# Output weights of twelve heads, the output bias and the first quad's queries moved from the attend block into the queries stage

## What is computed

```python
# layer 1; x is (16, 128, 512), context (16, 128, 512), 16 heads of 128
h = layernorm(x)
q = rms_norm(h @ q_w + q_b, nq_s)            # heads: "queries stage"
k = rms_norm(context @ ki_w + ki_b, nki_s)   # computed long before
v = context @ vi_w + vi_b                    # computed long before
p = softmax(q @ k.T / sqrt(128))             # per batch and head
x = x + (p @ v) @ o_w + o_b                  # o_w: 2048 x 512, sixteen heads
h = layernorm(x)
s = mean(abs(weight))
x = x + h @ (s * clip(round(weight / s), -1, 1)).T + bias
```

## Time and profile before

| | us |
|---|---|
| median of 3 runs | 1416.97 (1416.31 to 1417.77) |
| the profiled execution, its time | 1421.35 |
| its span, first to last instruction | 1419.6 |
| TensorE busy | 1335.0 (94%) |
| VectorE busy | 832.8 (59%) |
| ScalarE busy | 769.9 (54%) |
| GpSimd busy | 411.6 (29%) |
| mean granted TensorE clock | 0.966 |

### The profile page before, as it was taken

The page is one execution under the profiler, slowest core; times in us unless marked ns, Lnnn a source line. Parts: engine busy times, 40 slices in busy tenths (PEclk is TensorE's granted clock), DMA queues, the critical chain, the costliest instruction groups (busy, mean ns, idle before and its releaser), DMA issues. The chain is left out here.

```text
span 1419.6 us, 24647 instructions
## 1 busy us (share of the span) xinstructions
PE 1335.0 (94%) x7326; PEld 1117.0 (79%) x7327; DVE 832.8 (59%) x1575; ACT 769.9 (54%) x1890; POOL 411.6 (29%) x387
## 2 busy tenths in 40 slices
PE   6899989999999889989998989999958999999998
PEld 5688868888888767768886668888857888888887
DVE  2545533667676775354444458633258877777866
ACT  3325445788887542154446534545457566665661
POOL 0111023373739003559631054030056100000031
PEclk9999987999999999999999989999979999999999
DMA  6994479878787457476657877474446655556413
GB/s 231 357 350 163 147 236 294 283 247 292 260 268 254 174 141 289 178 227 179 198 144 238 282 237 228 110 243 147 158 146 165 167 157 165 159 162 164 119 45 119
DMA packets 175095, 288.33 MB, mean 203 GB/s; under 512 B 30176, under 2 KB 64736, under 8 KB 174752
## 3 DMA queue, kind: packets, MB, share of 16 engines
q1 hardware_dynamic: 149200, 231.78, 52.2%
q0 software_dynamic: 8672, 29.37, 6.4%
q10 hardware_dynamic: 17136, 26.09, 5.0%
HBM read 178.38 MB, written 108.80 MB: 202 GB/s over the span
## 5 line engine op out<-in xcount | busy, mean ns | idle before, releaser
L2778 ACT ACTIVATE attend_prob<-banks,attend_row,rq 128x128 f32<-128x128 f32 x256 | 113.7, 454 | 51.0 <-DVE attend_row L2853 50.9
L109 PE MATMUL banks<-of_shared_split,heads_wl 128*128 128x512 f32 x256 | 109.0, 426 | 9.2 <-ACT heads_ksq L1002 5.2
L109 PE MATMUL banks<-attend_wol,attend_ol 128*128 (+1 forms) x256 | 106.0, 414 | 0.0
L111 PE MATMUL banks<-of_shared_split,heads_wt 128*128 128x512 f32 x256 | 103.2, 403 | 0.0
L110 PE MATMUL banks<-of_shared_split,heads_wl 128*128 128x512 f32 x256 | 103.1, 403 | 0.0
L109 PE MATMUL banks<-queries_rows_split,queries_wl 128*128 128x512 f32 x256 | 100.8, 394 | 0.0
L111 PE MATMUL banks<-attend_wol,attend_ot 128*128 (+1 forms) x256 | 100.7, 393 | 0.0
L111 PE MATMUL banks<-queries_rows_split,queries_wt 128*128 128x512 f32 x256 | 99.8, 390 | 0.0
L110 PE MATMUL banks<-attend_wot,attend_ol 128*128 (+1 forms) x256 | 99.8, 390 | 0.0
L110 PE MATMUL banks<-queries_rows_split,queries_wl 128*128 128x512 f32 x256 | 99.7, 390 | 0.0
L2463 DVE TENSOR_TENSOR queries_total<-queries_total,queries_sq 128x512 f32<-128x512 f32 x60 | 41.6, 693 | 90.0 <-ACT queries_sq L2391 90.0
(11 more groups left out here) (374 smaller groups left out, 3660.9 us busy)
## 6 DMA issues: line engine op xcount, KB each, us to landing
mlstm_gmax<-running_max SPq DMA_DIRECT2D x36, 512.0 KB, 6.4
heads_raw<-in_L_xattn_ki_w SPq DMA_DIRECT2D x32, 512.0 KB, 6.4
k_heads<-heads_key ACTq DMA_DIRECT2D x64, 256.0 KB, 4.8
q_heads<-queries_head SPq DMA_DIRECT2D x64, 256.0 KB, 2.9
attend_q<-q_heads SPq DMA_DIRECT2D x64, 256.0 KB, 4.1
of_attend_k<-k_heads SPq DMA_DIRECT2D x60, 256.0 KB, 4.0
of_attend_v<-v_heads SPq DMA_DIRECT2D x60, 256.0 KB, 3.4
sorted_rows<-of_shared_split SPq DMA_DIRECT2D x2, 5120.0 KB, 30.0
```

What stands on the lines that cost most here:

```text
L109: nc.tensor.matmul(out, lead_l, lead_r, start=first, stop=False)
L111: return nc.tensor.matmul(out, trail_l, lead_r, start=False, stop=last)
L2778: ins = nc.scalar.activation(prob[:, j % 2, b, :], ps[:, j % 2, b * S:(b + 1) * S], ACT.Exp, bias=row[:, j % 2, 1, b:b + 1], scale=rq[:, b ...
```

## The change

Three pieces of work move from the start of the attend block into the queries stage.

The tile of the output weights becomes one, `wo`, with lead and trail of a head side by side, 2 KB apart, at the address of `rows_split`, the split normalised rows. These rows are free group by group as the last heads pass, and four heads of weights fit in the place of one group. So ScalarE copies two leads behind each of units 52, 53, 56, 57, 60 and 61, and VectorE makes two trails there (`CUTS`): twelve heads. Those of heads 12 to 15, in the place of the last group, are left in the attend block, in slots 4 to 7, with the trails on GpSimd.

GpSimd adds the output bias to all sixteen batches in the queries stage, batch b once 36 + b units are done. VectorE no longer waits for `bias_done` in the attend block.

SP loads the queries of the first quad at unit 54, into a tile `q_ahead` over places that the stage no longer uses; the first scores don't wait for a load.

```diff
@@ queries @@
+        CUTS = {}
+        for g in range(G - 1):
+            through = max(u for u, (h, of) in enumerate(UNITS) if of == g) + 1
+            CUTS[through], CUTS[through + 1] = (4 * g, 4 * g + 1), (4 * g + 2, 4 * g + 3)
...
                 if u == 54:
                     sp.wait_ge(wt_done, 2 * PAIRS)
                     load_ahead(3)
+                    sp.wait_ge(product, LAST[5] + 1)
+                    for k in range(HEADS_RING):
+                        sp.wait_ge(q_stored[k], 16 * len(range(k, 4, HEADS_RING)))
+                    for j in range(4):
+                        sp.dma_start(q_ahead[:, j, :], q_dram[j, :, 0:N]).then_inc(q_loaded, 16)
...
+            pool.wait_ge(staged, G)
+            pool.wait_ge(small_loaded, 16 * sum(late == 0 for *_, late in A.loads))
+            for b in range(B):
+                pool.wait_ge(product, BIASED + b)
+                nc.gpsimd.tensor_tensor(K.x[:, b, :], K.x[:, b, :], A.obias[:], ALU.add).then_inc(bias_done, 1)
+            pool.wait_ge(bias_done, B)
...
+                for i in CUTS.get(u, ()):
+                    act.wait_ge(wo_loaded, 16 * len(A.pieces))
+                    nc.scalar.activation(wo[:, i, 0], A.raw[:, i], ACT.Copy).then_inc(wo_lead, 1)
...
+                for i in CUTS.get(u, ()):
+                    dve.wait_ge(wo_lead, i + 1)
+                    nc.vector.tensor_tensor(wo[:, i, 1], A.raw[:, i], wo[:, i, 0].bitcast(F32), ALU.subtract
+                                            ).then_inc(wo_trail, 1)
@@ attend_and_last @@
-        wol = sb("wol", [P, H1, D], F32R)
-        wot = sb("wot", [P, H1, D], F32R)
+        wol, wot = wo[:, :, 0, :], wo[:, :, 1, :]
...
-            for j in range(4):
-                load_q(0, j)
             load_rkb(1)
...
-            for i in range(4):
-                cut(i)
-            bias(0)
-            for i in range(4, H1):
-                cut(i)
-            pool.wait_ge(wo_ready, QUADS)
-            pool.sem_inc(wo_ready, IT - QUADS)
-            for g in range(1, G):
-                bias(g)
...
-                    if isinstance(it, int) and it < 2:
-                        for i in ((4 + 2 * j, 5 + 2 * j), (12 + j,))[it]:
-                            weight_lead(i)
-
-            for i in range(4):
-                weight_lead(i)
+                    if isinstance(it, int) and it == 1:
+                        weight_lead(CUT + j)
+
...
-                if b == 0:
-                    dve.wait_ge(bias_done, (group(it) + 1) * GB)
...
-                pe.wait_ge(q_ring[j], (it + 1) * 16)
+                if not (isinstance(it, int) and it == 0):
+                    pe.wait_ge(q_ring[j], it * 16)
```

More of the change, by code:

```diff
@@ L2307, in _ @@
                     tile, rows_in = A.pieces[(u - 25) // 2]
[L2308 removed]
+                    sp.dma_start(tile, rows_in).then_inc(wo_loaded, 16)
                 if u == 44:
@@ L2317, in _ @@
                     load_ahead(3)
+                    sp.wait_ge(product, LAST[5] + 1)
[3 more added lines that the diff above has]
+                        sp.dma_start(q_ahead[:, j, :], q_dram[j, :, 0:N]).then_inc(q_loaded, 16)
                 sp.wait_ge(head_done, u + 1)
                 sp.dma_start(q_dram[h, :, g * N:(g + 1) * N], head[:, u % HEADS_RING, :]).then_inc(q_stored[u % HEADS_RING], 16)
-            sp.wait_ge(ahead_loaded, 16 * (len(A.loads) + len(A.pieces)))
+            sp.wait_ge(small_loaded, 16 * sum(late == 0 for *_, late in A.loads))
+            sp.wait_ge(ahead_loaded, 16 * sum(late > 0 for *_, late in A.loads))
+            sp.wait_ge(wo_loaded, 16 * len(A.pieces))
+            sp.wait_ge(q_loaded, 16 * 4)
             for k in range(HEADS_RING):
@@ L2611, in attend_and_last @@
         probT = sb("probT", [P, 2, N])
-        ol = sb("ol", [P, 2, 4, N], F32R)
         ot = sb("ot", [P, 2, 4, N], F32R)
         row = sb("row", [P, 2, 4, GB])
-        lead, trail = (w[:].rearrange("p (g c) n -> p g c n", g=G) for w in (wol, wot))
+        lead, trail = (w.rearrange("p (g c) n -> p g c n", g=G) for w in (wol, wot))
         ternT = q[:].bitcast(F32R)
```

52 lines of the change are left out of this document (31 added, 21 removed).

## The result

The changed kernel takes 1409.18 us (median of 10 runs, 1404.47 to 1413.34), the kernel before 1416.64 us (10 runs, 1413.53 to 1422.46). The ratio is 0.9948, with a 95% interval of 0.9933 to 0.9963: faster by 7.4 us, 5.2 to 9.5 us with the interval. The forecast was 1411.2 us, in a range of 1408.8 to 1414.2, and the measured median lies 0.4 us inside its lower end.

What follows compares the result with a forecast made beforehand. It took TensorE as the bound except in the 35.2 us from attend start to first output product, where it waits: 6.1 us gained there, 0.3 lost at the ternary step, so 1416.97 - 5.8 = 1411.2 us, range 1408.8 to 1414.2.

Steps and rivals of the forecast that it cites:

- The main step: Start of attend block to first output product: 29 us (28 to 30.5) instead of 35.2, a gain of 6.1 us.
- The wait for the queries: Start of the attend block: first scores wait for the scaled keys alone, not the queries' load, a gain of 2.2 us.
- Rival (d): Ramp: GpSimd did not stretch the slots, which stay at 4.5 us; gain 2.2 to 2.5 us, 1414.6 us; chance 0.09.
- First score to first transpose: Ramp, first score to first transpose of probabilities: 6.85 us becomes 6.0, less the product's excess of 0.86.
- The slots: Ramp, five slots between transposes: 3.7 us for the first, 16.0 for four, two of them at 4.3; 22.7 before.
- The ternary weights: Queries stage: a GpSimd bias addition delays VectorE's square and ternary step, costing 0.3 us, between 0 and 1.5.
- Rival (c): Queries stage: the ternary step loses twice to GpSimd and TensorE waits 1.5 us; 1412.4 us; chance 0.11.
- Nothing paid on ScalarE, VectorE and SP in the queries stage: Queries stage: moved copies, subtractions and query loads fit into idle time, cost zero; bound 1 us for the loads.
- Rival (a): Ramp: the clock stays at half all through, gain 4.5 us, 1412.5 us; chance 0.12.
- Rival (b): Ramp: the clock does not fall at all, slots 3.72 us, gain 7.8 us, 1409.2 us; chance 0.06.
- Rival (e): Output products: TensorE reads side-by-side lead and trail slower; slower by over 0.2% from 11 ns each, 1420.4 at 12; chance 0.04.
- TensorE's idle time before the transposes: Ramp: sign of the change working, TensorE's wait before transposes of probabilities falls from 11 us to under 6.

Runs made afterwards that it cites:

- e1: Changed kernel with the sixteen bias additions back in the attend block; first head of the queries stage to end 565.49 us, against 562.71 and 563.05 for the change.
- e2: Kernel before with only the early load of the queries (and the changed tiles); first head to end 569.30 us, again 569.27, against 569.33 and 568.58 before.
- e4: Changed kernel plus twelve idle GpSimd additions with two SBUF inputs at the start of the attend block; first head to end 565.81 us.
- e5: Changed kernel plus twelve idle GpSimd multiplications with one SBUF input at the start of the attend block; first head to end 564.37 us.
- e6: Changed kernel plus twelve idle GpSimd memsets, which only write, at the start of the attend block; first head to end 563.75 us.
- e9: Changed kernel with bias additions from unit 44 and first two heads' keys made in the queries stage; ratio 0.9958 to the kernel before, first head to end 561.59 us.
- e3: Changed kernel with the bias additions starting once 44 units are done instead of 36; first head to end 561.76 us.
- e7: Changed kernel plus idle matmuls, eight before the last sums and six before the first score; first head to end 563.04 us.

## Why the prediction was right, and where it was not

The forecast was a gain of 5.8 us; the stretches that the change touches give 6.1 us (5.5 to 6.6), and the timed runs 7.4 (5.2 to 9.5) and 4.2 (1.8 to 6.7). That the sum is so close is in part luck: by the means of two executions the ramp gave 6.9 us (38.1 to 31.3) where the forecast has 6.1, and the ternary step took 0.8 where it has 0.3. The main step held: the attend block's first instruction, a transfer that SP issues, stands at 1029.48 us, the first output product at 1057.52, so 28.0 us, where 29 (28 to 30.5) was forecast and 35.2 was before.

- **The wait for the queries, 2.2 us.** Right as a term of the whole: the keys, started at 1029.92, let the scores go at 1030.72, 0.8 us on. But it is no gain by itself. It needs keys that nothing holds: e1, with the weight split moved and the bias not, has the early queries and a hand-over of 7.34 us. And e2, where the keys are undisturbed, gives back behind the first scores what it wins before them. Rival (d) expected 2.2 to 2.5 us from the queries alone; e2 shows 0.
- **First score to first transpose, 6.0 us.** 5.98 us, twice.
- **The slots, 19.7 us.** 18.6 us, an over-estimate by 1.1. I had the floor of 3.72 us right, but gave two of the later four slots half clock. In both executions of the change the clock was up by slot 1. In e1, e4, e5 and e6 it was still at half there, in e9 at half again, and slots 1 and 2 were 3.9 to 4.3 and 4.1 us, about as I had assumed. So the term was mis-sized by something that differs from execution to execution, and the range of 4.8 to 7.2 us was the right answer to it.
- **The ternary weights, 0.3 us.** This was the under-sized step: 0.96 and 0.64 us. The argument failed where it said that VectorE's second step, standing back to back with the first, would not be held again. It was, for 1.04 us beyond the 0.80 of the first (in the second execution 1.04 beyond 0.44). It also had the additions come one a unit, where three were due at once. TensorE's wait there, 0.75 us, is over the 0.5 that was given as the bound. Rival (c) had this mechanism, and priced it at 1.5. e3 shows the cause, and that it could be had for nothing.
- **Nothing paid on ScalarE, VectorE and SP in the queries stage.** Right: from the first head to the last it is 183.51 us before and 184.46 after, and the difference is the ternary stall; e3, without that stall, has 183.50 with all copies, subtractions and loads in it. Stores held ScalarE at one head for 0.13 us in the change (unit 57), at two for 0.43 and 0.45 in e3, and in the kernel before at one for 0.67 (unit 53); TensorE doesn't wait for it.
- **Rival (a), half clock all through,** fell by the 3.72 us. **Rival (b), no fall at all,** fell by the scores of 3.78 us. **Rival (e)** fell by the output products:

```profile
L110 PE MATMUL banks<-wo,attend_ol 128*128 (+1 forms) x193 | 80.0, 415 | 0.0
```

That is the same 415 ns as in the earlier trace rows, with lead and trail side by side.
- **A sign that was wrong:** TensorE's idle time before the transposes was to fall from 11 to under 6 us. Its waits in the ramp (us in total, times, longest), after, then before:

```profile
PE banks L2987 <- DVE attend_prob L2878: 8.2, 6, 2.2
PE banks L2979 <- DVE attend_kn L2859: 3.1, 1, 3.1
```

```profile
PE banks L2972 <- DVE attend_prob L2862: 11.1, 5, 3.1
PE banks L2964 <- DMA attend_q<-q_heads: 5.6, 1, 5.6
```

It is 8.2 us, and yet the ramp is as short as it should be. At full clock TensorE's own work in a slot (2.44 us, 3.72 less the 1.28 of its wait) is shorter than 3.72 us, and what is missing is idle time before the next transpose. I had counted part of the slots at half clock, where TensorE fills them.

**Open.** Moving the weight split gave 3.8 us, 1.6 of them by the clock. How the other 2.2 are shared between ScalarE's copies and GpSimd's subtractions was not tried apart, and e4, where GpSimd works without the copies, has no slot near 4.5 us but by the clock. What makes the clock rise before slot 1 in one execution and only in slot 2 in another, or fall again in between, isn't known; only e7 had it at full from the first scores on, with idle matmuls right before them that cost as much as they won.

## What to carry to other kernels

When a wait ends earlier, ask what it then waits for and who disturbs that: the early queries alone were worth nothing, for the time went to a row scaling beside GpSimd and to a slot at lower clock. Work moved off a critical stretch onto GpSimd's free time should be placed by where VectorE has long steps with two SBUF inputs on a due date; here one constant, 36 or 44, was worth 0.6 to 1.0 us. And cut the traces at the first instruction that a change can touch, since of 16.8 us between two profiles only 6.6 belonged to it.

## What the hardware showed that I had not expected

- GpSimd operations with one SBUF input hardly hold VectorE (two keys 1.42 us, undisturbed 1.41, all in all 0.7 us), those with two hold it for most of their own length (2.92 us), those that only write not at all.
- Two VectorE steps back to back can both be held by GpSimd: 1.49 and 3.38 us instead of 0.69 and 2.34.
- What a hold costs depends on the step that it meets: a key step of 1.60 us instead of 0.74 cost nothing in e4, holds on a product and a scaling on the chain cost their full 1.1 us in slot 0 of the kernel before.
- TensorE's clock was at half level (1.2 GHz) for most or all of the first scores in every kernel but e7, with idle time of 1.3 to 5.6 us right before them. In e2 it fell again in slot 5, in both runs, after waits of 2.13 and 2.14 us ahead of that slot's transpose; after a wait of 2.15 us in the same place it did not fall in the first execution of the kernel before.
- One core with the same program has spans of 1402.7 to 1411.6 us, the three longest at a lower mean clock than the four shortest; between its two traces 7.6 of 7.9 us lie ahead of the stretch that the change touches.
